# First two sequences of a recurrent block: positions first, attention weights in four transfers, a signal per mix, decays as a column

## The reference, cut to what matters

```python
xx = q_shift_1d(x)             # first quarter of channels from the token before, second from the token after
xk = x * mix_k + xx * (1.0 - mix_k)      # the same for xv and xr
k = jnp.einsum('btc,oc->bto', xk, Wk)    # the same for v (xv, Wv) and r (xr, Wr)
def step(carry, kv):                     # ew = exp(w)
    a, b = carry
    kt, vt = kv
    eku = jnp.exp(u + kt)
    out = (a + eku * vt) / (b + eku)
    ek = jnp.exp(kt)
    return ((a * ew + ek * vt, b * ew + ek), out)
y = jnp.einsum('btc,oc->bto', jax.nn.sigmoid(r) * wkv_out, Wo)
x = _layernorm(x + y)
...
weights = (x @ router_w)[..., 0] + router_b[0]   # scores that choose the tokens of the second layer
```

## Time and profile before

| what | value |
|---|---|
| median of 3 runs | 769.72 us (769.6 to 769.82) |
| the profiled execution's own time | 775.65 us |
| its span | 773.9 us |
| mean granted TensorE clock, share of 2.4 GHz | 0.974 |
| busy: TensorE, its weight loads | 728.7, 539.3 us |
| busy: VectorE, ScalarE, GpSimd | 648.4, 515.7, 512.5 us |

### The profile page before, as it was taken

How to read it: one execution, slowest core, us unless ns; L and a number is a source line. 1 busy time by engine, 2 the same in 40 slices (tenths; PEclk the granted TensorE clock), 3 DMA queues, 4 the chain that set the end, 5 groups by cost and what they waited for, 6 DMA issues and landing times. The chain is left out here.

```text
span 773.9 us, 12972 instructions
## 1 busy us (share of the span) xinstructions
PE 728.7 (94%) x4334; PEld 539.3 (70%) x4334; DVE 648.4 (84%) x1326; ACT 515.7 (67%) x983; POOL 512.5 (66%) x495
## 2 busy tenths in 40 slices
PE   7899999999999999999988899988999998999993
PEld 5466666666666666676555676767787776899993
DVE  6798998989989899999999998787977677567784
ACT  3568888888888888888866674775656766632120
POOL 1687887878878778787667667855548773631333
PEclk9999999999999999999999999997999999999997
DMA  8012424233242332422322201234001120000001
GB/s 235 4 52 63 144 69 136 68 100 103 68 134 71 91 114 69 123 81 68 104 88 82 68 29 48 90 103 130 16 15 56 43 82 2 2 7 23 28 17 39
DMA packets 37336, 55.38 MB, mean 72 GB/s; under 512 B 3360, under 2 KB 26528, under 8 KB 37280
## 3 DMA queue, kind: packets, MB, share of 16 engines
q1 hardware_dynamic: 34464, 46.28, 19.6%
q0 software_dynamic: 2816, 8.39, 3.6%
HBM read 35.78 MB, written 18.87 MB: 71 GB/s over the span
## 5 line engine op out<-in xcount | busy, mean ns | idle before, releaser
L804 PE MATMUL ps<-halves 128*128 128x512 f32 x558 | 238.7, 536 | 0.0
L799 PE MATMUL ps<-arena,wa 128*128 128x512 f32 x384 | 204.5, 615 | 15.5 <-DVE arena L1591 6.9
L804 PEld LDWEIGHTS ps<-halves 128*128 128x128 f32 x558 | 107.5, 193 | 100.1 <-issue 91.6
L819 PE MATMUL ps<-wa,arena 128*128 128x256 f32 x512 | 131.7, 380 | 0.0
L605 POOL TENSOR_TENSOR arena<-arena 128x1024 f32<-128x1024 f32 x32 | 76.3, 2384 | 78.4 <-issue 54.9
L589 POOL TENSOR_TENSOR arena<-arena 128x512 f32<-128x512 f32 x93 | 116.4, 1281 | 5.5 <-ACT halves L1215 5.5
L799 PEld LDWEIGHTS ps<-arena,wa 128*128 128x128 f32 x384 | 71.0, 192 | 45.2 <-POOL halves L590 14.1
L1559 DVE TENSOR_TENSOR_SCAN arena<-ewb,ps 128x511 f32<-128x511 f32 x64 | 74.5, 1205 | 27.8 <-ACT ps L1187 26.9
L819 PEld LDWEIGHTS ps<-wa,arena 128*128 128x128 f32 x512 | 87.3, 190 | 6.6
L596 POOL TENSOR_TENSOR arena<-arena 128x1024 f32<-128x1024 f32 x32 | 76.2, 2380 | 22.5 <-ACT arena L1201 22.5
L1586 DVE TENSOR_TENSOR_SCAN arena<-ewb,ps 128x511 f32<-128x511 f32 x64 | 74.1, 1199 | 0.0
(11 more groups left out here) (233 smaller groups left out, 1511.0 us busy)
## 6 DMA issues: line engine op xcount, KB each, us to landing
arena<-x_chan SPq DMA_DIRECT2D x32, 512.0 KB, 4.2
out<-arena SPq DMA_DIRECT2D x32, 512.0 KB, 3.3
arena<-x_chan SPq DMA_DIRECT2D x64, 127.8 KB, 3.3
wa<-w_attn SPq DMA_DIRECT2D x1, 1024.0 KB, 7.2
wa<-w_up SPq DMA_DIRECT2D x1, 1024.0 KB, 6.1
wa<-w_down SPq DMA_DIRECT2D x1, 1024.0 KB, 5.5
wqk<-w_qk SPq DMA_DIRECT2D x1, 512.0 KB, 5.0
wv<-w_v SPq DMA_DIRECT2D x1, 256.0 KB, 5.2
```

Source lines behind the costliest of these rows:

```text
L799: mm(bank[:, o, :], wa[:, m, 0, out_part], xm[s.par][:, m, :], start=True, stop=False)
L804: last = mm(bank[:, o, :], w[:, m, out_part], x[s.par], start=False, stop=(t == 2))
L819: last = mm(psY[:, j, :], gg[s.par][:, c, tokens], wa[:, 3, c, :], start=False, stop=(c == CC - 1))
```

## The change

It touches the first two sequences and the operand of the scans.

- The positions are issued first, then the columns, then sequence 0. The router's row and bias come behind sequence 1.
- The attention weights come in four transfers of 256 KB, each with its own semaphore: k, v and r ahead of sequence 1, the output's behind it.
- `columns` has a semaphore of its own, for VectorE's mixes and ScalarE's exp(w).
- VectorE signals after each mix of sequence 0, and TensorE waits in that sequence for one weight and one mix before each projection. The output's weight is waited for before the first output.
- `keep_warm` runs 21 times instead of 18.
- The table `ewb` is no longer filled. The scans read exp(w) as one column, repeated along the row. Its room is kept under the name `shifted`, since the second layer uses it.
- In sequence 0 the clamp stands between the numerator's scan and its end, and the centring of the router's row behind the numerator.
- GpSimd no longer waits for the small transfers.

```diff
-            sp.dma_start(cols[:, :], columns).then_inc(small_in, 16)
-            sp.dma_start(rwb[:, :], router_w.rearrange("(a c) -> a c", a=1).to_broadcast([P, C])).then_inc(small_in, 16)
-            sp.dma_start(rbb[:, :], router_b.rearrange("(a c) -> a c", a=1).to_broadcast([P, 1])).then_inc(small_in, 16)
...
+            def load_weight(m):
+
+                sp.dma_start(wa[:, m, :, :], w_attn[m].rearrange("(c p) o -> p c o", p=P)).then_inc(w_in[m], 16)
+
             sp.dma_start(ptok[:, :], positions).then_inc(pos_in, 16)
+            sp.dma_start(cols[:, :], columns).then_inc(cols_in, 16)
             load_channels(At(0, 0))
-            sp.dma_start(wa[:, :, :, :], w_attn.rearrange("m (c p) o -> p m c o", p=P)).then_inc(w_in, 16)
+            for m in range(3):
+                load_weight(m)
             load_channels(At(0, 1))
+            sp.dma_start(rwb[:, :], router_w.rearrange("(a c) -> a c", a=1).to_broadcast([P, C])).then_inc(small_in, 16)
+            sp.dma_start(rbb[:, :], router_b.rearrange("(a c) -> a c", a=1).to_broadcast([P, 1])).then_inc(small_in, 16)
+            load_weight(3)
...
             pool.wait_ge(consts_made, 4)
-            pool.wait_ge(small_in, 3 * 16)
...
             def projections(s):
-                pe.wait_ge(mixed, s.n + 1)
+                if not is_start(s):
+                    pe.wait_ge(mixed, s.n + 1)
...
+                    if is_start(s):
+                        pe.wait_ge(w_in[m], 16)
+                        pe.wait_ge((first_mixed, scaled, mixed)[m], 1)
...
             def outputs(s):
                 pe.wait_ge(g_ready, s.n + 1)
+                if is_start(s):
+                    pe.wait_ge(w_in[3], 16)
...
-            keep_warm(7, 18)
-            pe.wait_ge(w_in, 16)
+            keep_warm(7, 21)
...
-            act.wait_ge(small_in, 3 * 16)
+            act.wait_ge(cols_in, 16)
             a.activation(euw[:, :, :], uw, ACT.Exp, scale=1.0 / T).then_inc(eu_made, 1)
             act.wait_ge(consts_made, 4)
-            act.wait_ge(w_in, 16)
+            for m in range(3):
+                act.wait_ge(w_in[m], 16)
...
-            dve.wait_ge(small_in, 3 * 16)
+            dve.wait_ge(cols_in, 16)
             dve.wait_ge(chan_in[0], 48)
...
-            for m, done in enumerate((None, scaled, mixed)):
+            for m, done in enumerate((first_mixed, scaled, mixed)):
...
-            for c in range(CC):
-                v.tensor_scalar(ewb[:, c, :], ewb[:, c, :], euw[:, 1, c:c + 1], None, ALU.mult).then_inc(ewb_made, 1)
...
-                    last = v.tensor_tensor_scan(bb[:, c, 1:T], ewb[:, c, 0:T - 1], psK[:, c, 0:T - 1], 0.0, ALU.mult, ALU.add)
+                    last = v.tensor_tensor_scan(bb[:, c, 1:T], euw[:, 1, c:c + 1].to_broadcast([P, T - 1]), psK[:, c, 0:T - 1], 0.0, ALU.mult, ALU.add)
...
-                    v.tensor_tensor_scan(aa[:, c, 1:T], ewb[:, c, 0:T - 1], psV[:, c, 0:T - 1], 0.0, ALU.mult, ALU.add).then_inc(scan_a_done, 1)
+                    v.tensor_tensor_scan(aa[:, c, 1:T], euw[:, 1, c:c + 1].to_broadcast([P, T - 1]), psV[:, c, 0:T - 1], 0.0, ALU.mult, ALU.add).then_inc(scan_a_done, 1)
...
+            def router_centred():
+
+                dve.wait_ge(small_in, 2 * 16)
...
-                    clamp_of(at)
-                    num_of(at)
+                    if is_start(at):
+                        num_scan_of(at)
+                        clamp_of(at)
+                        num_rest_of(at)
+                        router_centred()
+                    else:
+                        clamp_of(at)
+                        num_scan_of(at)
+                        num_rest_of(at)
```

More of the change, by code:

```diff
@@ L274, in rwkv_then_selected_block_kernel @@
         row_out = [sem(f"row_out{p}") for p in range(4)]
-        w_in = sem("w_in")
+        w_in = [sem(f"w_in{m}") for m in range(4)]
         w2_in = sem("w2_in")
+        cols_in = sem("cols_in")
+        first_mixed = sem("first_mixed")
         small_in = sem("small_in")
@@ L462, in tables_of, with is_start @@
             return 2 if 2 * first + 1 < MB else 1
+        def is_start(at):
+            return isinstance(at.n, int) and at.n == 0
         def pair(n):
```

26 lines of the change are left out of this document (11 added, 15 removed).

## The result

The changed kernel took 767.15 us (median of 20 launches, 763.11 to 771.42), the kernel before, launched in the same set, 770.11 (20 launches, 766.74 to 774.26). The ratio is 0.9956, with a 95% interval of 0.9938 to 0.9973. In a second set of launches the same two kernels stood at 764.08 (6 launches) and 770.66 (11 launches), 0.9913 with 0.9885 to 0.9941. The forecast of 765.0 against 769.72 was a ratio of 0.9939. Launches of one kernel spread over 8 us, twice what was at stake, so the reasons are read from where an instruction stands in a trace. Six profiles have the changed kernel's beginning unchanged up to the first product (after, e10, e4, e5, e6 and e7), and that product starts at 8.40 to 9.37, as the transfers land; the steps from there to the third sequence mostly repeat to about 0.2.

What follows compares the result with a forecast made beforehand. TensorE, gapless from the third sequence, bounds the kernel through its late start: 3.0 (first hole) plus 1.8 (slow K) less 0.1 (side entry) gives 4.7 off 769.72, so 765.0 us; own range 764.3 to 765.5, wide range 762.8 to 767.5.

Steps and rivals of the forecast that it cites:

- What bounds it: From the third sequence TensorE runs without a gap, so whatever moves its first instruction there moves the rest.
- The first hole: TensorE's 3.63 us idle between warm-up and first projection; the projection was to start 3.0 earlier, at 8.8.
- the slow K: First sequence's K block at a dropped clock, 5.23 us instead of 3.43; full clock was to save 1.8.
- The side entry: ScalarE's wait for GpSimd's second-sequence difference; channels had to land by 12.7, forecast 12.67, 0.1 us allowed.
- Clamp, router's row, column, table: VectorE's edits, each forecast worth 0; for the column, bounds of -7 to +7 ns a scan.
- the second hole: TensorE's 2.57 us idle between first and second sequence; forecast still 2.6, with the slow stretch behind it staying.
- the own range: The forecast's narrow range around 765.0, 764.3 to 765.5 us, given chance 0.47.
- A: Rival: the cut weight transfers don't overlap, second sequence starts 2.6 later; 772.3 us, slower; chance 0.04.
- D: Rival: the scans' decay column is dearer than read; gain gone from 0.15 us a scan over 32 scans; chance 0.03.
- E: Rival: the earlier start doesn't reach the end, something unseen holds the loop where it was; 769.7 us; chance 0.04.
- B: Rival: second sequence's channels or first weights come late by 0.5 to 1.8; 765.5 to 766.8 us; chance 0.22.
- C: Rival: slow clock stretches in or after the second sequence fall away, 763.2 us, chance 0.14; one added, 766.8, chance 0.06.

Runs made afterwards that it cites:

- e10: The changed kernel again, unchanged, with a second profile and five more rounds of launches; 764.08 us, ratio to the kernel before 0.9913.
- e4: The changed kernel plus 12 identity products behind the first sequence's projections, filling TensorE's second idle stretch; 764.79 us (12 launches), ratio to the kernel before 0.9937.
- e5: The changed kernel with a signal for each mix in the second sequence too; 765.78 us (12 launches), ratio to the kernel before 0.9948.
- e6: The changed kernel with decay table and clamp position as before, the router's centring staying behind the numerator's scan; 770.36 us (one launch).
- e7: The changed kernel plus two identity products in each period of the second layer's attention from the fourth on; 768.52 us (12 launches), ratio to the kernel before 0.9984.
- e3: The changed kernel with the four small transfers again ahead of the first sequence's channels, in their old order; 768.96 us (one launch).
- e2: The changed kernel with its attention weights again in one transfer of 1024 KB; 772.87 us (one launch).
- e9: The changed kernel with the first sequence's projections waiting for the last of the three mixes, as before the change; 767.65 us (one launch).
- e8: The kernel before, unchanged, profiled a second time; 771.24 us (one launch).
- e1: The kernel before with 35 instead of 18 warm-up products, filling TensorE's first idle stretch; 765.39 us (one launch).

## Why the prediction was right, point by point

**What bounds it.** Right. Both traces run the same 242.7 us from the third sequence to the twentieth's scan, and so do all ten others (242.6 to 242.8), so a gain at the beginning is kept in full up to there. Behind it the profiles scatter by 6.8 us whatever the kernel.

**The first hole.** Right in sum: 2.87 at the start (8.92 against 11.79, forecast 3.0) and the slow K. Either side of it is a draw: the changed beginning started at 8.40 to 9.37, and the weights of before landed at 11.0 to 12.1. The parts, each undone by itself, are 0.8 for the order of the loads (e3), 1.5 for the cut (e2) and 1.2 for the signals (e9), each uncertain by about 0.5 for the same reason, which overlap, since they are 3.5 together. The slow K, which I took at 1.8 from K's own length, is worth 1.80 in the one pair that differs in it alone (e8 against e1), and 1.65 of the 4.52 here.

**The step that was wrong.** "It ends at 8.16 + 0.66 = 8.8, after both first_mixed and the first weights." The warm-up ended at 8.20: 42 instructions took 6.60 us, where 36 had taken 6.56, because they went from 421 to 275 ns each at about 4.8, and before at about 6.3 (the profile's granted clock stands at 1.00 in both stretches). Its end scatters by itself, from 7.98 (e9) to 9.36 (e2) with the same 42. And first_mixed came at 8.7 instead of 8.1, because the channels landed at 7.2 instead of 6.57. I had carried their 3.6 to landing over unchanged; it was 4.2, and 3.7 to 4.4 in the other kernels with that order. The product follows the mix's end by another 0.2, which I had left out. The start came out at 8.92 all the same, by luck: what set it was the mix, late by about as much as I had thought the warm-up would cover, and the warm-up covers nothing from 8.2 on. The first weights, at 8.2, lay inside 7.6 to 8.5; in e6, which has the same transfers, they landed at 9.3 and set the start.

**The side entry.** Right to 0.1: landing at 12.8 or so, GpSimd's difference done at 14.54, ScalarE starting at 14.57. The 0.1 that I allowed for it was paid (14.57 against 14.49), but not to a late landing: the difference took 1.44 instead of 1.31, beside VectorE's remainder of the weights, as the last section shows. e6 shows the price once it is late, 0.46 for a difference that ended at 15.47.

**Clamp, router's row, column, table.** The column is worth nothing, as forecast (e6). e6 undid clamp, column and the rest of VectorE's edits together and lost 0.5 to a late transfer, so each of the others is worth nothing within that; one by one they were not undone.

**The sum.** Forecast 4.7. Between the two first profiles the third sequence moved by 4.52: 2.87 by the start and 1.6 by the slow K that fell away, with a slow K behind the second hole in both. Against e8, where the second K of before was fast, it moved by 3.3 only. In the launches it is 3.0 and 6.6 in the two sets, and 4.1 over both; the intervals are 2.1 to 4.8 and 4.5 to 8.9. So the size is confirmed at the beginning by the traces, and by the launches only as lying between 2 and 9. The forecast of 765.0 was missed by 2.15 in the first set, and with it the own range 764.3 to 765.5; 767.15 lies inside 762.8 to 767.5, near its upper end.

**The rivals.** A, D and E did not happen: transfers overlapped, the column cost nothing, the gain reached the loop. B did not happen in the two profiles of the changed kernel, but it did in e6's execution of the same transfers: first weights at 9.3, the second sequence's channels at 13.9 (beyond my 13.5), 0.45 at the start and 0.5 at the side entry. So it is a matter of the execution too. C was half right: whether a slow stretch stands behind the second hole is a matter of the execution (in six of the ten profiles that have the hole), and part of the late stretches is too. I gave it as an outcome of the change, but it happens to both kernels (before had it once and not the other time, the changed one twice), so it widens what is measured. With the old beginning the clock fell behind the second hole in one profile of three, with the new one in five of seven; whether the change makes it likelier, and so takes some of the gain back, is too few cases to say and stays open. "The three times of before lie within 0.22 us, which speaks against it" was the weak sentence: twenty launches of the same kernel lay 7.5 apart.

## What to carry to other kernels

Where an engine's first work waits for a load and for a chain on another engine, cut both, or neither pays: here either one alone left TensorE waiting until 10.2 to 10.5 instead of 8.9. An idle stretch ahead of TensorE's work like the ones of 2.2 to 4.4 us here may be paid twice, in itself and in a slow stretch behind it, and filling it with idle products costs one line (in e1 it took away a slow stretch of 1.8, more than a third of the 4.5). When launches scatter more than the change is worth, compare the place of one instruction ahead of the scatter, and don't read a difference of two profiled spans as the change's.

## What the runs showed of the hardware that I had not expected

**The same idle time, with and without a slow clock.** Behind second holes of 2.56 to 2.65 us the products ran at half the clock in before, after, e10, e2, e3 and e9 (0.57 or 0.58 granted over the 4 us in question), and at 1.00 behind 2.55 to 3.12 in e1, e7, e8 and e6. First holes of 0.2 to 1.3 never had it (seven cases), those of 2.18 to 4.36 always (three). The Trainium skill, TensorE: Matmul & The Clock Gate, section What's actually happening, has the change of clock varying from run to run; the traces agree.

**VectorE held up by GpSimd, and GpSimd by VectorE.** The router's row took 0.69 before (15.53 to 16.22) and 1.83 after the change (24.89 to 26.72), the same instruction. Before, GpSimd's difference ran from 14.76 to 16.07; after, its sum ran beside it:

```profile
24.21 2.35 POOL L605 TENSOR_TENSOR arena<-arena 128x1024 f32<-128x1024 f32 x1 [2.16 <-ACT arena L1216]
```

It ended at 26.56, and VectorE's instruction 0.16 behind it; before it was 0.15. In e1 nothing of GpSimd's ran beside the instruction (its difference had ended at 15.09), and it took 0.35:

```profile
16.82 0.35 DVE L1544 TENSOR_SCALAR rwb<-rwb,rwst 128x256 f32<-128x256 f32 x1
```

So it was held up in before too. The Trainium skill, SBUF — State Buffer, section SBUF: two separate sides, says that GpSimd and some of VectorE's instructions take one pair of ports in turn, for a whole instruction. All three cases agree with it, though no run was made to prove it. It cost nothing here, as VectorE was idle behind it; in front of a scan it would have been 1.5 us (1.83 - 0.35). In e6 it did stand in front of one: the rounding's remainder (L1559 there) took 1.91 instead of 0.95 beside GpSimd's difference, and the first scan started at its end.

The other way round, it sits in the side entry. In e9 the second sequence's channels were early, and GpSimd's difference started at 12.35, next to VectorE's remainder of the weights (12.37 to 13.32):

```profile
12.35 2.09 POOL L592 TENSOR_TENSOR arena<-arena 128x512 f32<-128x512 f32 x1 [9.45 <-DMA arena<-x_chan]
```

It took 2.09 instead of 1.3 and ended 1.12 behind VectorE's instruction. In after, e2, e3, e5, e7 and e10, where it started 0.03 to 0.64 behind the remainder's start, it ended 1.11 to 1.13 behind its end as well. So an earlier landing would not have ended it earlier. Before the change the remainder came behind the difference (16.25 against 14.76); the shorter beginning of VectorE has brought it in front.
